# Gated linear attention on one core: the outputs of a chunk as quarter-array products, with the scaling of the heads on GpSimd

## The reference

```
a = x + layernorm(attention(layernorm(x)))
out = a + layernorm(experts(layernorm(a)))

attention: q = relu(x Wq) (16 heads), k = relu(x Wk), v = x Wv (4 heads each), D = 64
           g = log_sigmoid(x Wg1 Wg2 + bg2) / 16
           S_t = exp(g_t) * S_{t-1} + k_t v_t^T;   o_t = (q_t / 8) S_t
           o = g_norm_weight * o * rsqrt(mean(o^2 over D) + eps);  result = o Wo
experts:   the best 2 of 8 by softmaxed router logits, each silu(x G^T) * (x U^T) times D^T
```

## Time and profile before

| | us |
|---|---|
| median of 3 runs | 1224.97 (1224.72 to 1226.8) |
| the profiled execution | 1229.17 |
| its span, first to last instruction | 1227.4 |
| mean granted TensorE clock | 0.984 of full |

### The profile page before, as it was taken

The page is one execution under the profiler, slowest core; times in us unless marked ns, Lnnn a source line. Parts: engine busy times, 40 slices in busy tenths (PEclk is TensorE's granted clock), DMA queues, the critical chain, the costliest instruction groups (busy, mean ns, idle before and its releaser), DMA issues.

```text
span 1227.4 us, 29645 instructions
## 1 busy us (share of the span) xinstructions
PE 1159.2 (94%) x9166; PEld 988.5 (81%) x9166; DVE 771.0 (63%) x2380; ACT 651.1 (53%) x1653; POOL 554.5 (45%) x686
## 2 busy tenths in 40 slices
PE   8999999999999999999999999399999999999995
PEld 5888878878878788888788788389999999988862
DVE  5777877887887787778778878423333333333337
ACT  4656656557547557557566573234444444443336
POOL 2344564554654654644645644423333333333326
PEclk9999999999999999999999999689999999999998
DMA  7010110100101100101101101334111111111534
GB/s 281 10 28 12 32 44 9 34 26 25 34 17 30 39 17 26 43 13 30 43 11 32 34 9 64 116 107 116 50 49 48 50 45 52 47 48 43 180 116 190
DMA packets 59677, 67.51 MB, mean 55 GB/s; under 512 B 6896, under 2 KB 49664, under 8 KB 59264
## 3 DMA queue, kind: packets, MB, share of 16 engines
q1 hardware_dynamic: 48720, 41.10, 10.7%
q0 software_dynamic: 8448, 17.45, 4.3%
q10 hardware_dynamic: 2480, 8.61, 2.2%
HBM read 37.98 MB, written 29.15 MB: 55 GB/s over the span
## 4 chain that ended last, share of the span: by engine, by line
PE 73%; DVE 13%; ACT 5%; issue 5%; DMA 3%; POOL 1%; DVEq 0%; ACTq 0%; SPq 0%; POOLq 0%
PE pO L779 10%; PE pO L606 6%; PE pJ L561 6%; PE pW L639 5%; PE pO L611 5%; PE pA L590 5%; PE pA L770 4%; PE pA L771 4%; PE pJ L770 4%; PE pJ L771 4%; PE pT L622 3%; PE pA L561 2%; PE pJ L532 2%; PE pA L539 2%; PE pJ L519 2%
## 5 line engine op out<-in xcount | busy, mean ns | idle before, releaser
L1658 POOL DMA_INDIRECT expert_out<-y,tail x136 | 130.1, 957 | 262.8 <-ACT y L1040 239.3
L890 ACT ACTIVATE sq<-pO 128x512 f32<-128x512 f32 x128 | 76.0, 593 | 170.3 <-PE pO L606 118.7
L606 PEld LDWEIGHTS pO<-vJ,aT 128*128 128x128 f32 x1024 | 127.9, 192 | 27.1 <-issue 24.0
L606 PE MATMUL pO<-vJ,aT 128*128 128x128 f32 x1024 | 139.1, 279 | 5.5 <-DVE aT L1176 5.5
L1569 POOL DMA_INDIRECT expert_rows<-x1n,rowi x120 | 120.3, 1002 | 48.0 <-issue 29.7
L779 PE MATMUL pO<-wdown_sb,vJ 128*128 128x128 f32 x1088 | 133.9, 277 | 0.0
L779 PEld LDWEIGHTS pO<-wdown_sb,vJ 128*128 128x128 f32 x1088 | 128.2, 194 | 0.0
L1183 DVE TENSOR_REDUCE ss<-sq 128x8 f32<-128x512 f32 x128 | 86.4, 675 | 62.1 <-ACT sq L890 61.2
L1437 DVE TENSOR_TENSOR vJ<-pA,kJ 128x256 f32<-128x256 f32 x136 | 57.6, 425 | 107.9 <-ACT kJ L1029 107.5
L611 PE MATMUL pO<-S_mid,qT 128*128 128x128 f32 x896 | 118.3, 275 | 0.0
L611 PEld LDWEIGHTS pO<-S_mid,qT 128*128 128x128 f32 x896 | 109.0, 192 | 0.0
(11 more groups left out here) (234 smaller groups left out, 2432.1 us busy)
## 6 DMA issues: line engine op xcount, KB each, us to landing
xt<-expert_rows SPq DMA_DIRECT2D x69, 130.0 KB
xa<-x SPq DMA_DIRECT2D x16, 256.0 KB, 3.1
xr<-x SPq DMA_DIRECT2D x16, 256.0 KB, 2.9
after_attention<-x SPq DMA_DIRECT2D x16, 256.0 KB, 2.4
arena<-after_attention ACTq DMA_DIRECT2D x8, 512.0 KB
expert_rows<-zeros SPq DMA_DIRECT2D x8, 390.0 KB
expert_out<-y,tail POOLq DMA_INDIRECT x136
wgate_sb<-wgate SPq DMA_DIRECT2D x1, 2048.0 KB, 9.9
```

The costliest lines, as they stand in the source:

```text
L606: last = mm(o[:, g, h, :, :], aT[:, c % 2, h, g * P:(g + 1) * P], vJ[:, c, h, :], start=(h == 0 and g == 0), stop=(c == 0), skip_group_che ...
L1658: g.indirect_dma_start(out=ys_dram, in_=y[:, k, :], in_offset=None, out_offset=bass.IndirectOffsetOnAxis(ap=tail[:, k, 1:2].bitcast(U32), ...
```

## The change

1. `outputs` becomes `first_outputs` (8 products of 64x64 weights against 64 columns, each on a quarter of the array) and `more_outputs` (8 more of the same kind, and for c > 0 another 16 with the state). A chunk has 32 such products in place of 8 of full size. The second group waits until the first is done (`first_psum`), since products on different rows of the array must not add to one bank at the same time. The result of a chunk takes half of both banks of pO, so there is one place for it in place of two: the first product of chunk c waits for `heads_ready`, the copy of chunk c-1.
2. ACT copies pO to `heads` (which lies in the unused half of S_mid) and then squares `heads`. The copy waits for `on_ready` of chunk c-2.
3. The scaling by rs moves from DVE to POOL (`head_apply`, 128x512, 8 in each turn). `norm_apply` and `router_norm` are cut into halves of two instructions, with a `head_apply` between them.
4. `out_transposes(c)` stands between the two groups of outputs of chunk c+2. Merges 0 and 1 stand behind the outputs of chunks 3 and 5, merges 2 and 3 among the keys, values and queries of the next sequence.
5. `norm_transposes` moves ahead of the outputs of chunk 2, `ranks` behind those of chunk 6. `vJ` and `S_mid` are no longer padded: `mids` writes 128x128 in place of 128x256, and own_step is gone.
6. ACT's and DVE's streams are reordered to match; on ACT the second gate function of half 0 and the router's rstd stand behind the head scale of chunk 2; on POOL the residual of tile 3 stands ahead of `norm_apply`.

```diff
-            def outputs(i, c):
+            def first_outputs(i, c):
                 pe.wait_ge(a_ready, i * NC + c + 1)
 
-                if c >= 2:
-                    pe.wait_ge(on_ready, i * NC + c - 1)
+                if c > 0:
+                    pe.wait_ge(heads_ready, i * NC + c)
                 else:
                     pe.wait_ge(raw_ready, i * (NC - 1) + NC - 1)
+                settle(pe)
+                for g in range(2):
+                    for r in range(2):
+                        for p in range(2):
+                            last = intra(c, p, 1 - p, g, r, g == 0)
+                last.then_inc(first_psum, 1)
+
+            def more_outputs(i, c):
+                pe.wait_ge(first_psum, i * NC + c + 1)
                 if c > 0:
                     pe.wait_ge(mid_ready, i * (NC - 1) + c)
...
             def squares(i, c):
                 act.wait_ge(o_psum, i * NC + c + 1)
-                a(sq[:, c % 2, :], pO[c % 2][:].rearrange("p k v -> p (k v)"), ACT.Square)\
+                if c >= 2:
+                    act.wait_ge(on_ready, i * NC + c - 1)
+                a(heads[:, c % 2 * 8:c % 2 * 8 + 8, :].rearrange("p (h k) d -> p h k d", h=2),
+                  head_bank.rearrange("p h (k d) -> p h k d", d=D), ACT.Copy).then_inc(heads_ready, 1)
+                act.wait_ge(heads_ready, i * NC + c + 1)
+                a(sq[:, c % 2, :].rearrange("p (n d) -> p n d", d=D), heads[:, c % 2 * 8:c % 2 * 8 + 8, :], ACT.Square)\
                     .then_inc(sq_ready, 1)
...
+            def head_apply(i, c):
+                pool.wait_ge(rs_ready, i * NC + c + 1)
+                settle(pool)
+                g.tensor_tensor(
+                    on[:, c % 2, :, :].rearrange("p k (h d) -> p h k d", d=D),
+                    heads[:, c % 2 * 8:c % 2 * 8 + 8, :].rearrange("p (h k) d -> p h k d", h=2),
+                    wide(rs[:, c % 2, :].rearrange("p (h k) -> p h k", h=2).unsqueeze(3), P, 2, 4, D),
+                    ALU.mult).then_inc(on_ready, 1)
```

More of the change, by code:

```diff
@@ L614, in outputs @@
+                if c > 0:
+                    for p in range(PAIRS):
+                        for g in range(2):
+                            for r in range(2):
+                                for h in range(2):
+                                    last = inter(c, p, h, g, r)
                 last.then_inc(o_psum, 1)
@@ L1169, in queries_and_states @@
                         state(j, n)
-                for c in range(4, NC - 1):
-                    state(j, c)
+                    for c in range(4, NC - 1):
+                        state(j, c)
             def mask(i, c):
@@ L1617, in turn @@
                     gate_relative(i + 1, 1)
+                head_apply(i, 5)
+                if more:
                     residual(i, 1)
+                head_apply(i, 6)
                 if routed:
@@ L1623, in turn @@
                         scatter(0, n)
+                head_apply(i, 7)
                 if more:
```

206 lines of the change are left out of this document (118 added, 88 removed).

## The result

The changed kernel takes 1426.12 us (median of four runs, 1422.36 to 1441.51), the kernel before 1225.88 in the same session: a ratio of 1.1656 with a 95% interval of 1.1569 to 1.1743. It is slower, as forecast, but by 200 us and not by 100, and 36 us above the range of 1205 to 1390. The profiled execution took 1422.36 us, its span is 1420.3 us, and the mean granted TensorE clock fell from 0.984 to 0.910.

The account below looks back on a forecast made before the run. PE's work was taken to bound the kernel; less product work and the keys' wait against three new waits gave +7.1 us a turn, +99 over 14 turns, about +103 in all: 1325 us, range 1205 to 1390.

Parts of the forecast that it names:

- The products: PE's output products as quarter products with mode changes and `first_psum` waits: 10.8 us against 13.3, 2.5 us less a turn.
- the sum: All terms of a loop turn added: -2.5 - 0.6 + 2.9 + 3.2 + 4.1 = +7.1 us; +99 us over 14 turns.
- GpSimd's price: Each `head_apply` of 128x512 on GpSimd takes 1.06 us, 8.5 us more a turn; bounds 0.62 and 1.28.
- First wait: PE at the transposes of xn, held by chunk 0's `head_apply` between GpSimd's normalisation halves: 2.9 us a turn.
- Second wait: PE at the router's transposes of x1n, behind chunk 2's copy, head scale, router's rstd and `head_apply`: 3.2 us a turn.
- Third wait: PE at the turn's end, for chunk 6's `head_apply` behind tile 1's residual on GpSimd: 4.1 us a turn.
- The keys' wait: PE's wait for a normalised merge ahead of the keys goes, since merges 0 and 1 come earlier: 0.6 us less.
- rival 2: TensorE's clock falls at each turn's end, costing 2 to 3 us a turn: 1360 us, 1350 to 1400; chance 0.17.
- Sharing between VectorE and GpSimd: VectorE's scans and small router instructions held up to 1.06 us each by GpSimd's; nothing summed, could add 1 us a turn.
- Rival 1: PE arrives later than the other engines, so waits stay under 1 us each: faster, 1165 to 1180 us; chance 0.18.
- Rival 3: Only half of the waits appear as other work moves in: 1215 to 1280 us; chance 0.10.
- rival 4: Quarter products on PE run one after the other: 26 us a turn, over 1400 us; chance below 0.01.

Follow-up runs that it names:

- z3_full_dve: Changed kernel with full-size output products in two PSUM places and the head scaling back on VectorE, ScalarE's copy and the orders kept; 1337.6 us.
- y0_dve: Changed kernel with only the scaling of the heads (`head_apply`) moved back from GpSimd to VectorE; 1316.8 us.
- x3_xn: Changed kernel with xn normalised whole ahead of chunk 0's scaling and its transposes moved behind chunk 2's outputs; 1397.7 us.
- z1_full: Changed kernel with full-size output products alternating between two PSUM places and a separate buffer for copied heads, orders and path as changed; 1394.0 us.
- y2_dve_router: Changed kernel with head scaling on VectorE, the router's rstd one chunk earlier on ScalarE and GpSimd normalising all router tiles first; 1295.7 us.
- z2_full_all: Changed kernel with full-size output products, xn and x1n each normalised whole, router's rstd earlier, and chunks 5 to 7 scaled earlier on GpSimd; 1302.0 us.
- x1_fill: Changed kernel with small bf16 filler products on TensorE ahead of its waits, results unused; 1394.5 us.
- w1_queued: Kernel before with eight unused 128x512 products added on GpSimd in `head_apply`'s places, each waiting until VectorE has scaled that chunk; 1274.4 us.

## Why the prediction was wrong in size

**The products** were right, but for 0.6 us: 2.5 us less a turn in the sum, of which 3.1 less busy and 0.6 waiting for `first_psum`. Measured, by the pair z3_full_dve and y0_dve in equal order, are 3.1 less busy, and by the timeline 0.38 + 0.27 us of waiting for `first_psum`. Against the kernel before, in its other order, the busy time at full clock is 2.5 us less (43.7 against 46.2).

**GpSimd's price** was right: 1.06 us forecast for `head_apply`, and in the groups by line of the changed kernel:

```profile
L1537 POOL TENSOR_TENSOR arena<-S_mid,rs 128x512 f32<-128x512 f32 x128 | 133.4, 1042 | 32.2 <-ACT rs L940 31.9
```

**First wait**, 2.9 forecast, 2.4 measured. GpSimd needed 4.15 us from the start of xn (318.91) as said, and counted from the start of chunk 0's scores (312.21; 311.02 before) it began as before, after 6.7 us. PE came later than I had it: 8.5 us after that start (320.75), forecast 7.8 to 8.2 (8.8 to 9.2 from 310.05). With 0.38 and 0.27 us of waiting for `first_psum`, chunks 0 and 1 saved next to nothing.

**Second wait**, 3.2 forecast, 2.5 measured. From the end of chunk 2's outputs (325.60) to x1n (333.1) are 7.5 us, forecast 7.6. PE's own work meanwhile was 4.9 and not 4.4 us, since two gate logits took 1.05 and 1.1 us and not 0.87 each behind quarter products.

**Third wait**, 4.1 forecast, 3.0 measured in two pieces (1.78 + 1.19). The chain of chunk 6 took 6.8 us (from 346.93 to the end of GpSimd's 352.69 + 1.04) and not 6.2; but PE had more to do, for chunk 7's products ran at half clock and filled part of the wait. The first piece is not of that chain at all: it ends with the scaling of chunk 5 (348.90 + 1.04), which stands behind `gate_relative` of half 1 (347.88), and this the forecast had only in a side remark.

**The keys' wait** went, 0.6 us, as said. **Not in the sum** were the queries' wait for `qT` (0.8 us a turn) and the second merge's for `oT` (0.75 us). Together 1.5 us, while the three waits came to 8.0 and not 10.2. With `first_psum` and the keys' wait all standing still was forecast at 2.9 + 3.2 + 4.1 + 0.6 - 0.6 = 10.2 us more than before and came to 9.7 (10.95 less 1.3), right within its error by two misses that cancel.

**The step that failed is the sum, which ran at full clock.** It added and removed microseconds of PE work at 2.4 GHz, and left the fall of the clock to rival 2, with a chance of 0.17, once a turn and at 2.5 us. The falls came in every turn of the loop, mostly two or three times, and cost 5.1 to 5.6 us a turn, 72 to 78 us in 14 turns (by the fillers and by the stretches; against y0_dve's 43.7 us the mean is 5.3). The argument against that rival, that work stands between the pieces of the wait, was no argument: PE was busy for 1.81 of 3 us in 352.60 to 355.60, and the clock stayed at 0.50. The stretch in the earlier trace rows, 1.07 busy of 2 us, had shown the same once; I took it for the rarity it was in a kernel that hardly ever waits. The place at the router's wait I did not consider at all. With the clock counted, the same sum gives 1325 + 14 x 5.3 = 1399. The 14 turns of the loop take 59.7 us each (70.92 to 907.30, from one batch of state updates to the same one 14 turns on) and took 47.5, which is 172 of the 193 us by which the two spans differ. Of the other 21, 3 stand ahead of the loop, where the forecast had 2; 12 in the last turn, where it had 0 to 3; and 6 in the experts' stage, whose work is the same. The last two weren't followed row by row.

**Sharing between VectorE and GpSimd** I put at nothing, and as a delay on VectorE it is there. From the changed kernel's VectorE timeline:

```profile
335.57 2.05 DVE L1153 TENSOR_TENSOR_SCAN arena<-in_chunk,arena 128x512 f32<-128x512 f32 x1 [2.72 <-POOL arena L1559]
...
343.57 1.02 DVE L1352 TENSOR_TENSOR pick<-cst,top_f 128x32 f32<-128x32 f32 x2
...
346.39 1.22 DVE L1153 TENSOR_TENSOR_SCAN arena<-in_chunk,arena 128x512 f32<-128x512 f32 x1
...
348.96 1.01 DVE L1365 TENSOR_SCALAR den<-ediff 128x4 f32<-128x4 f32 x1
```

GpSimd's scalings stand at 335.50 to 336.54, 343.38 to 344.44 and 348.90 to 349.94, and GpSimd is idle from 346.34 to 347.88. The same scan takes 2.05 us with a scaling beside it and 1.22 without, the two `pick` 1.02 us against 0.29 before, and `den` 1.01 us against 0.16 in the earlier trace rows; it ends 0.03 us behind the scaling. `den` is in the chain of chunk 6's scaling and more than makes up the 0.6 us over the forecast. What these delays cost in time was not tried apart.

**Rival 1** (faster) fell, for its condition, all three waits together under 3.1 us, was missed by 5 us. **Rival 3** (half of the waits) fell, as the three waits came to 8.0 of 10.2 us, and **rival 4** by the 36 ns of a quarter product. **Rival 2** was the right mechanism at half its price, and in one of its places only.

## What to carry to other kernels

In a kernel whose TensorE is busy throughout, a wait can be paid twice: once as time, and once as clock behind it. So price each new wait a second time with the work that follows at 1.2 GHz, here 10 us of waits and 5 of clock a turn, and look in the old trace for the one place where it already happens. Less work for TensorE need not be less time: the same 3.1 us a turn gained 21 us in one neighbour of this kernel and lost 18 and 32 in two others. Before moving a step to an idle engine, look at what stands behind it there and who waits for that; with order and path unchanged the same load cost 45 us, in its new place 109. And read a gain by its parts: x3_xn hit its forecast with the waits as long as before.

## What was not expected of the hardware

How easily the clock falls, and how little it follows one wait's length. In most turns of z1_full it falls once, behind a wait of 2.7 us for xn, and not behind one of 2.3 for x1n; z3_full_dve falls only at the end of a turn, behind 1.2 and 1.0 us, and not behind 1.7 and 1.3 us at xn and x1n; y0_dve, with the same waits at the end of the turn, falls there in every second turn. y2_dve_router and z2_full_all stand still for 7.6 us of 51.3 and 5.1 of 51.8 in a turn and do not fall in 120 to 720 us. Not even the direction is safe: of the three pairs with equal orders, the kernel that stands still for longer lost more clock in two and less in the third (y0_dve 10 us with 8.3 us of standing still a turn, z3_full_dve 18 with 6.2). Why one turn falls and the next doesn't stays open.

With more instructions PE can stand still without any other engine that the profile names. With 62 more in a turn (x1_fill, 844 against 782):

```profile
314.76 0.37 PE L601 MATMUL pA<-qT,kT 64*64 64x256 f32 x1 [1.15 <-issue]
...
323.28 0.70 PE L572 MATMUL pJ<-xnT,wq_sb 128*128 128x256 f32 x2 [1.72 <-issue]
```

What triggers it is open, and the kind of the added products (bf16, 256 columns) is not told apart from their number: the changed kernel has 782 instructions in a turn and stalls for 0.3 us only, and w1_queued, which leaves PE's program as before, shows 0.7 us a turn at the state updates against 0.3.

Quarter products with two chunks' results in separate places, which would need no copy, weren't tried: all eight banks are in use, and two chunks would have had to share a bank that PE writes while ScalarE or VectorE reads it.
